# The Hadamard products of a weight matrix, moved from a kernel's last third to its first projections

## The reference

```python
up_gate = jnp.einsum('bsd,hd->bsh', x, W1)
up_lin = jnp.einsum('bsd,hd->bsh', x, W3)
hidden = jax.nn.silu(up_gate) * up_lin
hidden = fwht(hidden)                      # Walsh-Hadamard over the 1024 hidden columns, / sqrt(1024)
out = jnp.einsum('bsh,dh->bsd', hidden, W2)
```

## Time and profile before

| | us |
|---|---|
| median of 3 runs | 705.83 (705.29 to 706.45) |
| span of the profiled execution | 704.5 |
| around the span (median less span) | 1.3 |
| first slots with layer norm of the input | 6 to 31 |
| tail of block 1's attention | 620 to 633 |
| feed-forward of block 1, from its first gate product | 633 to 700 |

### The profile page before, as it was taken

How to read it: one execution, slowest core, us unless ns; L and a number is a source line. 1 busy time by engine, 2 the same in 40 slices (tenths; PEclk the granted TensorE clock), 3 DMA queues, 4 the chain that set the end, 5 groups by cost and what they waited for, 6 DMA issues and landing times.

```text
span 704.5 us, 16401 instructions
## 1 busy us (share of the span) xinstructions
PE 692.6 (98%) x4540; PEld 626.0 (89%) x4540; DVE 541.3 (77%) x1698; ACT 453.1 (64%) x1794; POOL 357.4 (51%) x555
## 2 busy tenths in 40 slices
PE   8999999999999998999999999999999999999998
PEld 4789999999999997888888999999999999978887
DVE  6889999999999998968845666766777776796443
ACT  4888888888888875423156666666666666664221
POOL 5998888898898844002079832323232323016100
PEclk9999999999999999999999999999999999999999
DMA  6011110101021020000021010100101100000000
GB/s 238 2 47 50 57 47 2 46 0 45 1 105 60 0 76 22 25 1 0 16 90 61 13 50 21 41 29 31 44 15 58 46 0 0 0 2 0 1 31 31
DMA packets 8794, 24.78 MB, mean 35 GB/s; under 512 B 928, under 2 KB 2464, under 8 KB 8608
## 3 DMA queue, kind: packets, MB, share of 16 engines
q1 hardware_dynamic: 8304, 23.27, 9.5%
q10 hardware_dynamic: 432, 0.85, 0.3%
HBM read 23.07 MB, written 1.05 MB: 34 GB/s over the span
## 4 chain that ended last, share of the span: by engine, by line
PE 90%; DVE 5%; issue 2%; ACT 2%; POOL 0%; ACTq 0%; DVEq 0%; POOLq 0%
PE bank L508 12%; PE bank L500 11%; PE bank L398 11%; PE bank L899 11%; PE bank L527 7%; PE bank L412 5%; PE bank L366 5%; PE bank L430 5%; PE bank L359 4%; PE bank L435 4%; PE bank L973 3%; PE bank L450 3%; PE bank L977 2%; DVE x L665 1%; PE bank L993 1%
## 5 line engine op out<-in xcount | busy, mean ns | idle before, releaser
L665 DVE SCALAR_TENSOR_TENSOR x<-bank,rinv,x 128x256 f32<-128x256 f32 x256 | 123.0, 481 | 25.6 <-PE bank L398 23.4
L643 ACT ACTIVATE probs<-scores,negmax 128x128 f32<-128x128 f32 (+1 forms) x256 | 117.4, 472 | 6.6 <-DVE negmax L703 5.3
L544 ACT CAST turned<-bank 128x256 fp32r<-128x256 f32 x104 | 38.8, 373 | 102.6 <-PE bank L412 98.4
L784 POOL TENSOR_TENSOR a_hi<-raw_a,zero 128x384 fp32r<-128x384 f32 (+1 forms) x60 | 43.7, 728 | 84.8 <-PE bank L527 84.8
L302 POOL TENSOR_TENSOR ln_r<-ln_ve,neg_half 128x1 f32<-128x1 f32 x26 | 17.0, 654 | 120.1 <-DVE ln_ve L276 120.1
L676 DVE TENSOR_TENSOR enc_lo<-bank,enc_hi 128x256 fp32r<-128x256 f32 x128 | 54.1, 423 | 29.4 <-PE bank L366 20.8
L684 DVE TENSOR_TENSOR turned<-bank,turned 128x256 fp32r<-128x256 f32 x104 | 43.7, 420 | 40.1 <-ACT probs_t L545 40.1
L398 PE MATMUL bank<-b_hi,enc_hi 128*128 128x256 f32 x256 | 73.5, 287 | 0.5 <-DVE x L665 0.5
L398 PE MATMUL bank<-b_lo,enc_hi 128*128 128x256 f32 x256 | 72.4, 283 | 0.0
L398 PE MATMUL bank<-b_hi,enc_lo 128*128 128x256 f32 x256 | 72.4, 283 | 0.0
L802 POOL TENSOR_TENSOR rot_a<-rot_a,rot_b 128x384 f32<-128x384 f32 x64 | 64.8, 1012 | 8.4 <-DVE rot_b L774 6.8
(11 more groups left out here) (179 smaller groups left out, 2395.4 us busy)
## 6 DMA issues: line engine op xcount, KB each, us to landing
raw_a<-in_wa SPq DMA_DIRECT2D x10, 768.0 KB, 4.4
raw_a<-in_wa SPq DMA_DIRECT2D x9, 512.0 KB, 3.5
raw_b<-in_wb SPq DMA_DIRECT2D x16, 256.0 KB, 2.6
hid_last<-in_wax SPq DMA_DIRECT2D x2, 512.0 KB, 4.7
w_a<-in_w2t SPq DMA_DIRECT2D x1, 1024.0 KB, 5.8
raw_b<-in_wdown SPq DMA_DIRECT2D x2, 512.0 KB, 3.4
x<-in_x SPq DMA_DIRECT2D x3, 256.0 KB, 4.7
raw_a<-in_wa ACTq DMA_DIRECT2D x1, 512.0 KB, 3.7
```

The source lines that it names most:

```text
L643: nc.scalar.activation(probs[:, c % 4, c0:c1], scores[:, c % 2, c0:c1], ACT.Exp, bias=negmax[:, c % 2, r:r + 1], scale=-1.0, accum_out=row ...
L665: nc.vector.scalar_tensor_tensor(out=x[:, m % 8, :], in0=output_bank(m)[:, hh * D:(hh + 1) * D], scalar=rinv[:, u, r:r + 1], in1=x[:, m % ...
```

## The change

The size-128 products come first, on the raw weights, and the butterflies behind them. The products stand between the first projections of block 0, the evictions with them; the load of w2 is in two halves, the first with `had` on ScalarE's queue in the first microseconds, the second on SyncE's queue behind the first loads. The products use banks 0, 1, 5 and 0, so the first two scores wait for evictions (4 and 2), and the first turned probabilities for the third. The butterflies stay in their slots, now end in `w2_b`, and the pieces are split from it.

```diff
         s_ident, s_rope, s_mask = sem("identity_loaded"), sem("rotation_loaded"), sem("masks_loaded")
-        s_scl, s_w2 = sem("scales_loaded"), sem("w2_loaded")
+        s_scl, s_w2 = sem("scales_loaded"), [sem(f"w2_loaded{i}") for i in range(2)]
         s_zero, s_half, s_scq = (sem(n) for n in ("zero_set", "half_set", "qscale_made"))
...
                 b, hh = u // 2, u % 2
+                if L == 0 and it is None and c < 2:
+                    pe.wait_ge(s_hadev, 4 if c == 0 else 2)
                 need(pe, s["max"], it, 2 * c - 2, 2)
...
                 need(pe, s["exp"], it, 2 * m + 2, 2)
+                if L == 0 and it is None and m == 0:
+                    pe.wait_ge(s_hadev, 3)
                 need(pe, s["ptev"], it, m)
...
                     pe.wait_ge(L["max"], 2 * UNITS)
-                    if f == 1:
-                        pe.wait_ge(s_hadev, 4)
                 elif i == 1:
...
+        HAD_BANK = (S_BANK, S_BANK + 1, PT_BANK, S_BANK)
+
         def pe_hadamard(pe, q):
...
-            pe.wait_ge(at[1]["max"], 2 * UNITS)
-            pe.wait_ge(s_bf, 6)
-            pe.wait_ge(s_had, 16)
-            if q >= 2:
-                pe.wait_ge(s_hadev, q - 1)
-            pe.matmul(bank[S_BANK + q % 2][:, :], had, w2_b[:, 2 * q:2 * q + 2, :].rearrange("p a d -> p (a d)"),
+            if q == 0:
+                pe.wait_ge(s_had, 16)
+            pe.wait_ge(s_w2[q // 2], 16)
+            if q == 2:
+                pe.wait_ge(ln["lo"], 2)
+            elif q == 3:
+                pe.wait_ge(s_hadev, 1)
+            pe.matmul(bank[HAD_BANK[q]][:, :], had, w2_a[:, 2 * q:2 * q + 2, :].rearrange("p a d -> p (a d)"),
                       start=True, stop=True).then_inc(s_hadmm, 1)
...
             act.wait_ge(s_hadmm, q + 1)
-            nc.scalar.mul(w2_a[:, 2 * q:2 * q + 2, :].rearrange("p a d -> p (a d)"), bank[S_BANK + q % 2][:, :],
+            nc.scalar.mul(w2_a[:, 2 * q:2 * q + 2, :].rearrange("p a d -> p (a d)"), bank[HAD_BANK[q]][:, :],
                           float(HID) ** -0.5).then_inc(s_hadev, 1)
...
                 eng.wait_ge(L["op"], UNITS - 8 * (1 - slot))
-                eng.wait_ge(s_hadev, 4)
+                eng.wait_ge(s_bf, 6)
                 a = 4 * slot + src // D
-                source = w2_a[:, a:a + 2, :].rearrange("p a d -> p (a d)")
+                source = w2_b[:, a:a + 2, :].rearrange("p a d -> p (a d)")
                 dst = b_w[slot]
...
             if c == 5:
-                nc.gpsimd.wait_ge(s_w2, 16)
+                nc.gpsimd.wait_ge(s_hadev, 4)
                 nc.gpsimd.wait_ge(ff[0]["hs"], 16)
...
             sp.dma_start(cst[:, 768:1536], consts[:, 768:1536]).then_inc(s_mask, 16)
-            sp.dma_start(had, consts[:, 128:256]).then_inc(s_had, 16)
             for L in range(2):
...
                     load(None, 1)
+                    sp.dma_start(w2_a[:, 4:8, :].rearrange("p a d -> p (a d)"), w2t[:, 4 * D:8 * D]).then_inc(s_w2[1], 16)
                 else:
...
                     load(it, 5)
-                if L == 0:
-                    sp.dma_start(w2_a[:, :, :].rearrange("p a d -> p (a d)"), w2t).then_inc(s_w2, 16)
                 load(None, 8)
...
             act.dma_start(cst[:, 256:768], consts[:, 256:768]).then_inc(s_rope, 16)
+            act.dma_start(had, consts[:, 128:256]).then_inc(s_had, 16)
+            act.dma_start(w2_a[:, 0:4, :].rearrange("p a d -> p (a d)"), w2t[:, 0:4 * D]).then_inc(s_w2[0], 16)
             act.wait_ge(raw_as[0][0], 16)
...
                         nc.scalar.copy(a_w[1][0][:, cs], raw_a[:, 1, cs]).then_inc(at[0]["ahi"], 1)
+                    if L == 0 and -4 <= c < 0:
+                        act_hadamard(act, c + 4)
                     elif L == 1 and c == -2:
...
                         ln_act(act, 2 * L + 1, t - 2, PJ_BANK + t % 2)
-                    if L == 1 and 2 <= t < 6:
-                        act_hadamard(act, t - 2)
                     if L == 1 and t >= 5:
...
                     if L == 0 and c == -4:
+                        pe_hadamard(pe, 0)
                         for t in (2, 3):
                             ln_pe(pe, 0, t, 4 + t)
+                        pe_hadamard(pe, 1)
+                    elif L == 0 and c in (-2, -1):
+                        pe_hadamard(pe, c + 4)
                     elif L == 1 and c == -3:
...
                 def tail(t):
-                    if L == 1 and 1 <= t < 5:
-                        pe_hadamard(pe, t - 1)
                     if 1 <= t < 5:
```

## The result

The changed kernel takes 708.84 us (median of 5 runs, 708.54 to 709.55), the kernel before 705.79 beside it: ratio 1.0044, 95% interval 1.0031 to 1.0056. It is 3.05 us slower; 1.4 were forecast, and 708.84 lies just above the range. Two more sets of runs gave 3.85 and 3.23 us.

What follows compares the result with a forecast made beforehand. The prediction took VectorE to bound the tail and TensorE mostly to set the head's time from 19.50 us. Head 2.34 - 0.83 = 1.5, less 0.1 in the tail, gave +1.4 us: median 707.2 us, range 705.2 to 708.7.

Steps and rivals of the forecast that it cites:

- steps 4 to 6: Head, products 2 and 3: first scores 2.34 us later, 0.83 us given back, so 1.5 us slower.
- Step 1, the tail: Second attention block's tail, 623 to 640 us: VectorE sets the time, so removing four products and evictions gains 0.1 us.
- The rival that the tail pays: Tail: VectorE's periods follow TensorE's outputs and shrink by 0.86 us each, giving 703.9 us; chance 0.10.
- The rival of the clock in the emptied tail: TensorE's clock falls in the half-empty tail and slows the gate products from 632.95: +1.1 us, 708.3 us; chance 0.10.
- a fall near 630: Sign of being wrong: TensorE's clock falling near 630 us, in the emptied tail.
- Step 2: Head: products 0 and 1 fit into TensorE's waits between the first projections, cover 0.27 and 0.19 us; cost 0.
- Step 3, loads, "Cost 0": Head: the moved loads fit the idle DMA slice from 7 to 8 us; cost 0, up to 1 us if late.
- Steps 4 and 5, "2.34 us later": Head: product 2 moves unit 2's head transposes from 21.03 to 21.7; product 3's eviction moves first scores from 21.39 to 23.73.
- Holding the clock: Head: TensorE's clock no longer falls with 1.7 us more work there; gives 0.3 us, used for product 2's start.
- Step 6, 0.83 given back: Head: 0.73 us returns between the projections of units 5 and 7, and 0.1 from small waits around 30 us.
- The span: Whole program: the profiled span of 704.5 us is 1.3 under the median, so a new span of 705.9 means 707.2.

Runs made afterwards that it cites:

- after_third: The changed kernel measured once more, unchanged, against the kernel before: 709.00 us, ratio 1.0047, 3.23 us slower.
- half_ahead: Changed kernel with the load of w2's second half ahead of the masks on SyncE's queue: 708.95 us, ratio 1.0043 to the kernel before.
- tail_without_products: Kernel before with the four products and their evictions left out of the tail, that part not computed: 705.92 us, ratio 1.0004 as printed, difference -0.14 us.
- without_last: Changed kernel without product 3 and its eviction, that part not computed: 707.62 us, ratio 1.0025 to the kernel before.
- first_two_only: Changed kernel without products 2 and 3 and their evictions, all loads kept: 705.86 us, ratio 1.0001 to the kernel before.
- late_evictions: Changed kernel with products 2 and 3 in other banks and their evictions one slot later on ScalarE: 707.28 us, ratio 1.0018 to the kernel before.

## Why the prediction was wrong

The places were right: every product, eviction and wait stands where the steps put it, and the two late products with their evictions carry the head's cost, as forecast. What failed is the sum, first of all steps 4 to 6: forecast 1.5 us for the head, measured 2.25.

- *Step 1, the tail.* Right that it is VectorE's; the 0.1 us isn't seen. The rival that the tail pays is dead (-0.14 us).
- *The rival of the clock in the emptied tail* is not dead. It was given 0.10 and 1.1 us; the clock fell there in two of the twelve profiles with an emptied tail (after_third, half_ahead), and cost 0.7 us in each. The prediction had named a fall near 630 as a sign of being wrong. It isn't the cause of the 3.05 us: executions with a mean clock under 0.999 are 7 of 15 in the three sets of the changed kernel, 38 of 94 in the kernel before, where the one profile that has it shows it in the head. What the head keeps of its clock the tail may lose again.
- *Step 2.* Right: products 0 and 1 are free (ratio 1.0001).
- *Step 3, loads, "Cost 0".* This fell. One instruction less on SyncE put 0.2 to 0.3 us behind the outputs. And the second half was late in one of five profiles of the changed kernel (0.63 us): there the rotation tables landed 7.3 us after their issue, and SyncE waits for them with the half behind it. The slice from 7 to 8 us, idle before, is full with the moved loads, but they don't make the tables late as a rule: 4.7 to 7.3 us in thirteen profiles (6.1 in the middle one), 5.8 to 6.2 in the five without. The step had weighed the Trainium skill's DMA: Bandwidth & Descriptors (Queues, rings and completion order), by which the engines take turns between queues; the wider scatter would fit that, a steady delay isn't seen.
- *Steps 4 and 5, "2.34 us later".* The main miss: at equal clock the scores go from 7.41 to 10.32, **2.91**. Of the 0.57 that are missing, 0.37 come from the profile that was counted from: its clock had fallen, so its scores stood at 7.78. Holding the clock was booked as the change's gain, and four of the eight profiles without products 0 and 1 have that gain too. The other 0.20 are a walk that was too short (23.73 less 13.61 is 10.12). The forecast starts were met all the same (21.7 and 23.73; 21.70 and 23.77), by luck: unit 2's projection began 0.16 us sooner. Of the 2.91, 1.68 are product 3's, as forecast. Product 2's are 1.23 (heads of unit 2 from 7.02 to 8.25 behind unit 2's projection) and not 0.67: at full clock the squares of unit 3 stood ready 5.43 us behind that projection (19.05 less 13.62 in tail_without_products), in the shown profile 5.84, and go to 6.70.
- *Step 6, 0.83 given back.* 0.66 (2.91 less 2.25). No wait of GpSimd and VectorE was counted; without_last has one where 1.2 us become 1.55.
- *The span.* 1.3 us around it were assumed from one span and another's median. Some 1.8 us lie around it in the kernel before, in each set, and 1.9 to 2.0 in the changed one; the execution profiled first was slower than the median by about 0.5.

Sum: 2.25 in the head, 0.3 at the end and 0.1 to 0.2 around the span make about 2.7, where 1.4 were forecast. Of the other 0.3 to 1.2 us in the three sets, late weights are one part, seen in one profile, and how many executions of a set lost their clock is another: at a mean clock of 1.000 the second and the third set both differ by 3.2 us. The rest, some 0.5 us, is open: from unit 7's projection to the last residual additions of the tail single executions differ by 1.1 us with the clock full in all of it (606.0 in first_two_only, 607.1 in late_evictions), which no run here was made to explain.

## What to carry to other kernels

Work is moved for nothing only if the engine that evicts it also has a hole there: ask of each moved matmul what stands behind its eviction in the in-order queue of ScalarE, and give it a bank that nobody wants soon. Before a step of under 1 us is priced from one profile, look at more profiles of the same kernel: what differs between them, here TensorE's clock, is not the change's to win in full, and what filling one place keeps, emptying another can lose. Where an engine's work in a stretch fits into the time of another that is full there, as TensorE's in VectorE's tail, taking work from it buys nothing, however busy the page calls it.

## Of the hardware, not expected

- The length of SyncE's instruction stream sets the end of the program by up to 0.8 us: 4.06 to 4.92 us from the last additions to the end, with 76 to 81 instructions as the expectations count them. The outputs are then issued in 2.05 us for 1.81, or the end lies later with none of them late. In the DMA traffic one instruction packet moves with it: at 76 it falls at the very end of the span or just behind it, at 77 about 1 us ahead of the end, at 78 and 80 2.0 and 2.5 us ahead, among the outputs, and at 81 there is none in the last 8 us. The Trainium skill's Runtime: NRT & Kernel Launch (Instruction fetch mechanics) has an engine's instructions refilled in blocks, at a cost mostly hidden. That what the end pays here is such a refill is argued, not shown.
- TensorE's clock fell in some executions of a kernel and not in others: at 13 to 18 us, and in the tail at 633 or 635 us, once behind the same 0.73 of 2.00 us busy at which it held elsewhere. A fall in the tail cost 0.7 us.
- A low part on VectorE took 1.22 and 1.24 us for 0.41 beside GpSimd's addition, depending on which of them began first by 0.1 us.
